# Adapter, attention and mixture of experts on one core: bias rows as products, bank copies on ScalarE, new step orders, later ring loads

## What is computed

```python
down = einsum(x, down_project * dg + db);  x0 = x + einsum(relu(down), up_project * ug + ub)
h = rmsnorm(x0) * attn_norm_w
q, k, v = split(h @ qkv_w + qkv_b)          # 16 query heads, 4 key and value heads of 64
q, k = rope(q), rope(k)
y = softmax_with_sink(mask(q @ k.T / 8)) @ v
x2 = x0 + (y @ proj_w + proj_b)
h2 = rmsnorm(x2) * ffn_norm_w
gw, topi = softmax(top_k(h2 @ gate_w + gate_b, 4))          # 4 of 32 experts
y2 = sum over chosen experts e:  gw * ((silu(g) * u) @ W_down[e]),  u, g = halves of h2 @ W_up[e]
out = x + x2 + y2
```

## Time and profile before

| | |
|---|---|
| median of three runs | 980.65 us (976.25, 980.65, 982.19) |
| profiled execution | 978.0 us |
| its span, first to last instruction | 976.0 us, mean granted clock 0.979 |
| busy in the span | PE 921.6, VectorE (DVE) 804.2, ScalarE (ACT) 523.1, GpSimd (POOL) 542.5 us |

### The profile page before, as it was taken

How to read it: one execution, slowest core, us unless ns; L and a number is a source line. 1 busy time by engine, 2 the same in 40 slices (tenths; PEclk the granted TensorE clock), 3 DMA queues, 4 the chain that set the end, 5 groups by cost and what they waited for, 6 DMA issues and landing times.

```text
span 976.0 us, 21879 instructions
## 1 busy us (share of the span) xinstructions
PE 921.6 (94%) x7434; PEld 742.7 (76%) x7434; DVE 804.2 (82%) x1808; ACT 523.1 (54%) x1246; POOL 542.5 (56%) x507
## 2 busy tenths in 40 slices
PE   7989899989999999898988999999999999999998
PEld 3657676776867678676753888888888888888887
DVE  5989799999999989998864777777777877777777
ACT  3144463836557374573750666665666666566641
POOL 3647558897888778787565233433343334343340
PEclk9989999999999899999998999999999999999999
DMA  8789889798897978879249877777867759663798
GB/s 276 195 258 306 277 260 288 242 303 264 278 306 242 291 242 286 253 264 276 92 147 347 269 246 278 246 252 253 285 218 284 256 188 317 232 231 108 249 394 303
DMA packets 127447, 251.41 MB, mean 258 GB/s; under 512 B 18756, under 2 KB 66122, under 8 KB 126797
## 3 DMA queue, kind: packets, MB, share of 16 engines
q1 hardware_dynamic: 83436, 186.79, 57.8%
q0 software_dynamic: 13776, 34.64, 9.8%
q10 hardware_dynamic: 30128, 28.58, 9.6%
HBM read 135.64 MB, written 102.12 MB: 244 GB/s over the span
## 4 chain that ended last, share of the span: by engine, by line
PE 57%; DVE 15%; POOL 9%; issue 6%; DMA 5%; ACT 4%; SPq 3%; ACTq 0%; DVEq 0%; POOLq 0%
PE gbank L1034 11%; PE scores L1034 11%; PE scores L1053 5%; PE gbank L1053 5%; DVE ring L1486 5%; PE gbank L904 5%; POOL lists L717 5%; DMA rows_in<-lists 2%; PE gbank L1097 2%; PE gbank L821 2%; DVE entry L1596 2%; PE scores L1008 2%; PE gbank L1008 2%; PE gbank L1043 2%; PE scores L1043 2%
## 5 line engine op out<-in xcount | busy, mean ns | idle before, releaser
L739 POOL DMA_INDIRECT pick_rows<-rows_out,pair_i x159 | 158.7, 998 | 265.6 <-ACT rows_out L1310 262.2
L724 POOL TENSOR_TENSOR ring<-ring 128x512 fp32r<-128x512 f32 x96 | 123.5, 1297 | 64.1 <-ACT ring L1245 63.8
L717 POOL DMA_INDIRECT lists<-put_rows,slot_i x112 | 108.8, 972 | 54.8 <-issue 29.8
L1034 PE MATMUL scores<-ring,in_part 128*128 x480 | 132.6, 412 | 1.5 <-DVE in_part L1726 1.5
L1034 PE MATMUL gbank<-ring,in_part 128*128 x474 | 129.8, 409 | 0.0
L821 PE MATMUL gbank<-h_t,w_qk 128*128 128x512 f32 x480 | 117.8, 399 | 1.6 <-ACT ring L1189 0.7
L904 PE MATMUL gbank<-w_o,ring 128*128 128x256 f32 x512 | 116.5, 381 | 1.8 <-ACT ring L1189 1.7
L1245 ACT ACTIVATE ring<-ring 128x512 fp32r<-128x512 f32 x96 | 59.5, 627 | 108.9 <-DMA w_parts<-ring 74.6
L1486 DVE SCALAR_TENSOR_TENSOR ring<-gbank,b_qk,rope 128x512 f32<-128x512 f32 x160 | 107.9, 743 | 3.8 <-PE gbank L821 3.5
L904 PEld LDWEIGHTS gbank<-w_o,ring 128*128 128x128 f32 x512 | 95.2, 191 | 14.2 <-ACT ring L1189 2.7
L821 PEld LDWEIGHTS gbank<-h_t,w_qk 128*128 128x128 f32 x480 | 88.8, 188 | 22.6 <-ACT ring L1189 1.1
(11 more groups left out here) (214 smaller groups left out, 1930.2 us busy)
## 6 DMA issues: line engine op xcount, KB each, us to landing
w_parts<-ring SPq DMA_DIRECT2D x192, 256.0 KB, 4.0
ring<-w_parts SPq DMA_DIRECT2D x32, 1536.0 KB, 7.7
rows_in<-lists ACTq DMA_DIRECT2D x159, 136.0 KB, 3.8
ring<-in_W_up SPq DMA_DIRECT2D x64, 256.0 KB, 4.4
picks<-pick_rows SPq DMA_DIRECT2D x6, 2048.0 KB, 13.9
ring<-in_W_down SPq DMA_DIRECT2D x32, 256.0 KB, 4.3
q_r<-rot SPq DMA_DIRECT2D x16, 512.0 KB, 6.4
q_r<-ring SPq DMA_DIRECT2D x16, 512.0 KB, 6.7
```

What stands on the lines that cost most here:

```text
L717: e.indirect_dma_start(out=lists, out_offset=bass.IndirectOffsetOnAxis(ap=slot_i[r % NPAY][:, s * TOPK + k:s * TOPK + k + 1], axis=0), in_ ...
L724: e.tensor_tensor(lower, lower.bitcast(F32), upper.bitcast(F32), ALU.subtract).then_inc(s_lower, 1)
L739: e.indirect_dma_start(out=pick_rows, out_offset=bass.IndirectOffsetOnAxis(ap=pair_i[:, i:i + 1], axis=0), in_=rows_out[i % NY][:, :], in_ ...
L1034: ins = e.matmul(front[i % FRONTS], in_parts[i % IN_BUFS][x][:, c, :], ring[:, bass.ds(at + y * WE + c * 2 * DFF, 2 * DFF)], start=k == 0, ...
```

## The change

The bias rows of `v` and of the projection are no longer added by VectorE. They are split into three rounded parts, which stand in partitions 0, 1 and 2 of `b_v` and `b_o` with zeros below (by columns of the identity), and one more product with a matrix of ones adds them into the bank. ScalarE then copies the bank out. All step lists are new; `BUSY[5]`, the fill ahead of the plan, is 20 instead of 30. The loads of experts 1 to 3 into the ring wait until all list puts have landed, and ScalarE's first `turn_in` stands two row loads earlier.

```diff
-BUSY = (11, 14, 24, 14, 20, 30, 40)
+BUSY = (11, 14, 24, 14, 20, 20, 40)
 ORDERS = {
...
-        turn_prob value attend down project turn_prob score attend up project
+        turn_prob attend down value value project turn_prob score attend up project
...
-    b_v = sb1("b_v", [P, KV * DH])
-    b_o = sb1("b_o", [P, D])
+    b_v = sb1("b_v", [P, KV * DH], F32R)
+    b_o = sb1("b_o", [P, D], F32R)
...
-        (b_v[:, :], d["b_v"]), (ident[:, :], d["ident"]),
+        (whole_b[0], d["b_v"]), (ident[:, :], d["ident"]),
...
         w.wait_ge(s_proj, NT)
+        for t in sorted(max(u for u in range(NT) if put_at[u] == b) for b in range(NPUT + NLATE)):
+            w.wait_ge(*listed(t))
         for n in range(1, RING):
             load_expert(n)
...
         def value(t, banks):
+            w.wait_ge(s_bias, 1)
+            e.matmul(bank[:, 0:KV * DH], ones_r[:, :], v_rows, start=True, stop=False)
             for k, (c, x, y) in enumerate(CHUNK_PRODUCTS):
...
-                               start=k == 0, stop=k == len(CHUNK_PRODUCTS) - 1)
+                               start=False, stop=k == len(CHUNK_PRODUCTS) - 1)
...
+            w.wait_ge(s_bias, 2)
+            e.matmul(bank[:, 0:D], ones_r[:, :], o_rows, start=False, stop=False, skip_group_check=True)
             w.wait_ge(s_y, 2 * t + 2)
...
-        def project(t):
+        def value(t, banks):
+            w.wait_ge(s_v, t + 1)
+            if t >= 2:
+                w.wait_ge(s_pv, t - 1)
+            e.activation(v_s[t % 2][:, :], gbank[banks[0]][:, 0:KV * DH], ACT.Copy).then_inc(s_v_s, 1)
+
+        def project(t, banks):
+            w.wait_ge(s_proj, t + 1)
...
+            e.activation(x2[m % 2][:, s, :], gbank[banks[0]][:, 0:D], ACT.Copy).then_inc(s_x2, 1)
...
         for i in range(AHEAD, ROWS_AHEAD):
+            if i == ROWS_AHEAD - 2:
+                turn_in(0)
             load_rows(i)
-        turn_in(0)
...
+            w.wait_ge(s_w_split, len(chunks))
+            bias_rows(whole_b[0], v_rows)
+
+        def bias_rows(bias, rows):
+            first, second, left = bias_parts
+            part = own.mark(e.tensor_copy(first.bitcast(F32R), bias))
+            w.wait_ge(s_vector, part)
+            part = own.mark(e.tensor_tensor(left, bias, first, ALU.subtract))
...
+            e.scalar_tensor_tensor(out=rows, in0=left, scalar=ident[:, 2:3], in1=second, op0=ALU.mult,
+                                   op1=ALU.add).then_inc(s_bias, 1)
 
         def constants():
             w.wait_ge(s_late, LATE)
+            w.wait_ge(s_middle, MIDDLE)
+            w.wait_ge(s_bias, 1)
+            bias_rows(whole_b[1], o_rows)
...
-        def value(t, banks):
-            e.tensor_tensor(v_s[t % 2][:, :], gbank[banks[0]][:, 0:KV * DH], b_v[:, :], ALU.add).then_inc(s_v_s, 1)
...
-        def project(t, banks):
-            e.tensor_tensor(x2[m % 2][:, s, :], gbank[banks[0]][:, 0:D], b_o[:, :], ALU.add).then_inc(s_x2, 1)
```

More of the change, by code:

```diff
@@ L109 @@
-        softmax_a up
+        cond down weights split up sums split apply split split split split split down split split
+        softmax_a value up
     """, """
-        turn_prob split softmax_a attend split sums split split apply project split turn_prob split
-        split softmax_a split attend split split turn_prob softmax_a project split attend split down
-        turn_prob split project split attend split softmax_a split split project up split
+        turn_prob value split softmax_a attend split sums split apply split project split turn_prob
@@ L114 @@
+        split softmax_a split split split attend split turn_prob softmax_a value project split value
+        split attend down split split project turn_prob split value attend split softmax_a project
+        split up split
     """, """
-        route_turn turn_prob route_turn softmax_a attend split sums split route_turn apply softmax_a
-        project turn_prob split root route_turn pack split split attend split split split project
-        split route_pick pack split turn_prob softmax_a attend tag tag turn_prob down project attend
@@ L118 @@
-        softmax_a split split pack tag up project tag pack
+        route_turn turn_prob route_turn value softmax_a attend sums softmax_a route_turn apply
+        project split route_turn split turn_prob split root split split value pack attend split
+        split pack split softmax_a route_pick project turn_prob split attend tag split value value
+        down project tag turn_prob attend split softmax_a pack project tag split up pack tag
     """, """
-        route_turn turn_prob route_turn root softmax_a attend route_pick pack route_turn softmax_a
@@ L121 @@
[L121 to L124, removed]
+        route_turn route_turn turn_prob root attend softmax_a root route_pick route_turn value
+        softmax_a project turn_prob route_turn tag pack attend value pack tag pack route_turn
@@ L125 @@
+        route_pick pack project turn_prob route_turn softmax_a attend tag root value pack tag
+        project route_turn turn_prob route_pick pack attend root tag route_pick project tag
+        route_turn root route_pick pack tag pack tag
     """),
     "POOL": ("""
-        split split split split pair split pair pair up pair pair split split split split up
+        split split split split split pair pair pair split pair split up pair split split up
     """, """
-        split split split split split split split pair split split pair split pair pair pair split
+        split split split split split pair split pair split split split pair split pair split pair
@@ L1267, in scalar_program @@
             elif name == "project":
-                project(k)
+                project(k, banks)
+            elif name == "value":
+                value(k, banks)
             elif name == "root":
@@ L1627, in vector_program @@
                 pair(*k, banks)
-            elif name == "value":
-                value(k, banks)
             elif name == "softmax_a":
@@ L1633, in vector_program @@
                 softmax_b(k)
-            elif name == "project":
-                project(k, banks)
             elif name == "route_pick":
```

101 lines of the change are left out of this document (53 added, 48 removed).

## The result

The changed kernel takes 994.4 us (median of four runs, 991.6 to 998.0) beside 980.3 (976.3 to 982.2): a ratio of 1.017, 95% interval 1.013 to 1.021. Forecast were 971 and a range of 961 to 986.

| stretch | before | after | change | forecast |
|---|---|---|---|---|
| start, to group 1's first sums (L808, after: L813) | 67.6 | 80.1 | +12.5 | +3.8 |
| from there to group 2's (pass of group 0) | 58.3 | 62.1 | +3.8 | 0 |
| groups 1 to 5 | 293.0 | 290.8 | -2.2 | -8.7 |
| group 6's sums to the landing of the last put | 114.0 | 109.0 | -5.0 | -3.7 |
| landing to the third tile's expert products | 10.8 | 16.3 | +5.5 | +1.2 |

What follows compares the result with a forecast made beforehand. TensorE was taken as the bound, its longest wait being ahead of `attend`. From 978.0 us: start +3.8, groups 1 to 5 -8.7, group 6 -1.0, step to stage two -1.5, giving 970.6, predicted as 971; range 961 to 986.

Steps and rivals of the forecast that it cites:

- Net +3.8: Start: fourteen bias instructions add 5.9 us, less two early value adds, less a shortened stall, plus part of another.
- upper bound of 10.6: Start: most the bias rows could cost, 5.9 us and a second stall of 4.7.
- the stall of 4.74 us: Start: two tiny `w_gate` scalings on VectorE take 4.74 us until GpSimd's run ends; one 1.25 us split less there.
- 0, with 1.3 either way: Group 0: the added products and the `value` step cost nothing, being absorbed in TensorE's wait; bounds 1.3 us either way.
- the 4.01 us wait: Group 0, before the change: TensorE's wait for rotated queries on their way by DMA, taken to absorb the added work.
- 53.92 + 1.31: Passes of groups 1 to 5: TensorE's busy time in group 2, 53.92 us, plus 1.31 for the added products.
- 0.74 + 0.5 + 0.4: TensorE's waits per pass, in us: ahead of `attend`, for VectorE ahead of a score, for ScalarE ahead of a `value`.
- a wait of equal size takes the place: Rival: `attend` gets its operand but the next `turn_prob` or score is late; 976 us, chance 0.27.
- gain of 8.7: Groups 1 to 5: each pass 56.87 us against 58.61, 1.74 less, 8.7 us over five passes.
- Which I let give back 1.2: Step to stage two: last put 2.7 us faster, loads now beside first row loads give back 1.2, net -1.5.
- The upper bound of +0.2: Step to stage two: worst case, the first rows take as much longer as the last put did.
- bank copies stuck behind splits: Slower rival: ScalarE's split waits for its store while a finished `value` or projection fills a bank; 987 us, chance 0.15.

Runs made afterwards that it cites:

- experiment 6: Changed kernel with the start lists of before and all fourteen bias instructions moved behind the mask at the end of `constants`: 988.0 us.
- experiment 3: Changed kernel with the start lists of before on TensorE, ScalarE, GpSimd and SyncE, bias rows kept: 986.0 us.
- experiment 5: Changed kernel with the start lists of before and one bias instruction in place of each seven: 983.0 us.
- experiment 8: Changed kernel's products, three-part bias rows and ScalarE bank copies in the lists of before throughout, ring loads early: 988.2 us.
- Experiment 9: Changed kernel with one bias instruction for each seven, and SyncE's first store of a third moved behind the next two loads: 989.1 us.
- experiment 4: Changed kernel with one bias instruction in place of each seven, all lists as changed: 994.1 us.
- experiment 10: Changed kernel with the repeated pass's last pair step moved ahead of a projection (TensorE) and of the routing count (VectorE): 999.4 us.
- the three pairs: Profiles with against without the added wait ahead of the ring loads, on three kernels: the later loads cost 1.2, 3.1 and 3.4 us.
- experiment 1: Changed kernel without the added wait ahead of the ring loads of experts 1 to 3: 991.4 us.
- experiment 7: Changed kernel with old start lists, bias instructions behind the mask, and no added wait ahead of the ring loads: 987.9 us.
- experiment 11: Changed kernel with one instruction per bias row, lists of before up to the end, new end lists, ring loads early: 976.7 us.

## Why the prediction was wrong

*The start: the step that failed most.* "Net +3.8" was +12.5, beyond its own upper bound of 10.6. The fourteen instructions were priced right (5.9 us, experiment 6). What was wrong is what they meet and what they hide. Ahead of `h_t` they leave TensorE idle for 3.4 us, and its pair products then take 15.78 us instead of 14.36 (experiments 3 and 5; in experiment 8 the wait was 1.9 us and nothing was lost behind it). In the changed kernel the granted clock behind the 4.3 us wait is 0.50, the level of 1.2 GHz:

```profile
36.00:40.00 4.00, 3.99 (x10) 2.59 (x10) 2.13 (x3) 0.00 (x0) 0.17 (x1) 0.50 1.00 329
```

I had charged lost clock to the passes and never to the start. Nor did the stall of 4.74 us get shorter by the split of 1.25 that I took off: it moved from the scaling of `w_gate` to the first cast, with 4.54 us (4.72 in experiment 3), and the other bias instructions follow behind it.

By the Trainium skill (SBUF — State Buffer, "Who interferes with whom") a VectorE cast in a two-port mode or an instruction with two inputs in SBUF, on the one side, and a GpSimd instruction that reads SBUF, on the other, shut each other out. The traces agree on both sides: the cast ends at 58.42, GpSimd's last pair operation at 58.26; and GpSimd's split of 7.03 us, with others of 1.3, lies under VectorE's unbroken row of such instructions from 21.5 to 27.5.

*The start: the step that was missing.* The second path, the new start lists, was not in the sum at all. I had read the new order on TensorE and VectorE and priced one split less; I had not followed SyncE's list, where a store now stands ahead of two loads. That wait passes on from engine to engine: VectorE holds GpSimd's split, that holds SyncE's store, that the next load, that ScalarE's split, that the copies to `h_t`. Experiment 9 shows the price of the store's place with one step moved (4.9 us), experiment 4 that the new lists cost their full price without the bias work. The other 5.9 us of the lists were not taken apart; GpSimd's five splits ahead of its first pair are on the chain.

*Group 0.* "0, with 1.3 either way" was +3.8. I let the 4.01 us wait of the earlier trace rows absorb the added work. It did not: TensorE is busy for 54.5 us there instead of 53.2, the score waits 6.0 us for the queries' move instead of 4.0, a `turn_prob` waits 1.6 us for a bank of `attend`, and two waits of 1.1 us together are gone. That the new lists alone bring the move later is likely but not shown: the score waits 4.0 to 6.6 us in the nine profiles with the new pass of group 0, and 4.1 and 5.1 in the two with the old one and the added products. The wait of `turn_prob` exceeds 0.5 us in three of the nine.

*The passes.* Three terms held: 0.7 us ahead of `attend` for 0.74, TensorE busy for 54.9 us where 53.92 + 1.31 was forecast, no drop of the clock. The step that failed is the sum of waits, 0.74 + 0.5 + 0.4: measured 3.1 a pass (15.5 / 5), because the score's wait for moved queries and the pair's for a bank are new. It is the rival "a wait of equal size takes the place", and it named the rotated queries; I gave it 0.27. Of the -2.2 that remain, the waits gave 0.9 (16.4 to 15.5); the rest goes with a clock that no longer falls, TensorE being busy for 274.7 us in the five passes instead of 276.7 (the earlier trace rows added up), products included. But a gain of 2.2 us is within the scatter: the eight profiles with the new pass lists (experiment 10 aside) take 290.8 to 296.3 us for the five passes, the two with the old program 291.3 and 293.0. What all eight show is the score's wait, 6.1 to 9.8 us in sum, and no gain of 8.7. Experiment 8 has passes of 57.9 us without the new place of `attend`; experiment 10 shows that the new wait can't simply be moved off.

*Group 6 and the last put.* -5.0 for -3.7: the landing gave 3.1 for 2.7, the rest about 2 for 1.

*The step to stage two.* "Which I let give back 1.2" was +5.5 in the trace, so together with the put a loss. The right bound was the row's own: a put that took 2.7 us longer beside three loads of 1.5 MB. The first row loads stand in that place now, several of them, one behind the other on the chain. From the start of the last put to the third tile's products it is 18.7 us for 16.3: +2.4 where -1.5 was forecast, and inside the 1.2 to 3.4 of the three pairs. The pair on the changed kernel itself gives 1.2 of it. The kernels with early loads and the new place of the turns (experiments 1, 7, 8 and 11) take 16.3 to 17.6 us, so that place costs 1.3 at the most. The upper bound of +0.2 doesn't come out of the row either: 2.7 given back for 2.7 gained is 0.

By the Trainium skill (DMA: Bandwidth & Descriptors, "Issuing engines are not separate DMA queues") the row loads of ScalarE's queue share their engines with SyncE's ring loads. The trace agrees: 5.43 and 9.59 us, in windows with a DMA share of 0.99 and 1.03:

```profile
544.00:548.00 4.00, 0.43 (x2) 0.29 (x2) 0.00 (x0) 0.00 (x0) 0.00 (x0) 0.84 0.99 390
548.00:552.00 4.00, 1.68 (x7) 1.23 (x6) 0.71 (x4) 1.30 (x5) 0.00 (x0) 0.50 1.03 413
```

The rival that was slower, bank copies stuck behind splits (987), had the direction right but not the reason: over five passes TensorE waited 0.8 us ahead of a value's bias product.

## What to carry to other kernels

Where a change comes with a new order, follow the queue of every engine through it, SyncE's above all: a store that waits for a slow engine holds each load behind it, and here, in a start where TensorE had nothing else to do, that cost 4.9 us. When two paths are late at once, removing the shorter shows next to nothing and removing the longer only the difference; removing each, and both, tells their prices (80.1, 79.6, 76.2, 68.8 here, give or take 1 us or more). And an engine relieved of 3.3 us a pass gives nothing where TensorE waits for something else next: list those waits over all passes before counting the gain.

## What the runs showed of the hardware that I had not expected

In the start, GpSimd and VectorE did not take turns instruction by instruction: the one that came second waited for the whole unbroken run of the other, 4.5 to 4.7 us for a single cast of 128x256 (0.29 alone) and 7.03 us for a split (1.3 alone). And three loads of 1.5 MB did not become free by being moved: beside the last put they cost it 3.1 to 3.7 us, and beside the first row loads they brought the third tile's products, counted from the put's landing, 4.9 to 6.8 us later (three pairs).
